# Scan layers: B's diagonals by DMA instead of DVE, bias and residual added by DVE out of PSUM

## The reference

```python
proj = seq @ W_proj.T + b_proj                    # x_in, delta, B, C
delta = softplus(delta + dt_bias);  A = -exp(A_log)
h = exp(d_t[..., None] * A) * h + (d_t * x_t)[..., None] * b_t[:, None, :]   # for every pixel t
y_t = einsum('bdn,bn->bd', h, c_t)
out = (y + x_in * D) @ W_out.T + b_out
x = x + out
```

## Time and profile before

| | |
|---|---|
| median of the runs | 4305.36 us |
| the profiled execution: span, first to last instruction | 4308.6 us |
| PE busy | 3710.7 us, 86% |
| DVE busy | 3432.3 us, 80% |
| POOL busy | 2659.4 us, 62% |
| ACT busy | 2105.8 us, 49% |
| DVE: diagonals (1160) | 454.0 us, 128 instructions |
| DVE: scans (1136) | 944.3 + 887.2 us, 1536 instructions |
| PE: scan inputs (818) | 865.7 us, 24576 matmuls |
| PE: sums over states (831) | 798.1 us, 3072 matmuls |
| transfers, mean of the span | 97 GB/s |

### The profile page before, as it was taken

One profiled execution on the slowest core, in us unless ns is written; L12 is line 12 of the kernel. 1 busy time (PEld: TensorE's weight loads), 2 busy tenths in 40 slices (PEclk: granted clock), 3 DMA queues, 4 the chain that ended last, 5 costly groups with the idle time before them and its releaser, 6 DMA issues.

```text
span 4308.6 us, 119610 instructions
## 1 busy us (share of the span) xinstructions
PE 3710.7 (86%) x49136; PEld 2266.0 (53%) x49136; DVE 3432.3 (80%) x3492; ACT 2105.8 (49%) x2803; POOL 2659.4 (62%) x973
## 2 busy tenths in 40 slices
PE   4994899899999996789889888899898888888897
PEld 4994666666666664344444444444444444444443
DVE  6564567667576663699998998999999989999997
ACT  2331343444444443556555555555565555555563
POOL 1111121111211210599899999999999999999998
PEclk9997899999999998799999999999999999999999
DMA  9624142242332330553543543544535535435433
GB/s 101 85 44 108 54 124 81 85 119 70 95 109 69 105 91 25 120 116 79 125 106 83 125 102 92 125 94 103 122 84 120 112 79 124 109 79 130 103 87 83
DMA packets 296948, 416.40 MB, mean 97 GB/s; under 512 B 31369, under 2 KB 185741, under 8 KB 296385
## 3 DMA queue, kind: packets, MB, share of 16 engines
q1 hardware_dynamic: 295440, 408.35, 41.7%
q10 hardware_dynamic: 978, 0.34, 0.0%
HBM read 267.09 MB, written 91.16 MB: 83 GB/s over the span
## 4 chain that ended last, share of the span: by engine, by line
PE 27%; DVE 16%; issue 12%; ACT 3%; POOL 1%; DVEq 1%; DMA 0%; ACTq 0%; POOLq 0%
DVE ssm_h L1136 11%; PE ssm_u_ps L818 10%; PE ssm_y_ps L831 10%; PE ssm_scratch L848 4%; DVE ssm_b_diag L1160 3%; PE ssm_scratch L858 1%; DVE ssm_stats L1143 1%; POOL ssm_h L1216 1%; ACT ssm_decay L967 1%; PE ssm_u_ps L893 1%; DVE ssm_y_sb L1165 1%; ACT ssm_xn L994 1%; PE ssm_scratch L873 1%; PE ssm_scratch L867 0%; DVEq L1128 0%
## 5 line engine op out<-in xcount | busy, mean ns | idle before, releaser
L1216 POOL TENSOR_TENSOR ssm_h<-ssm_h,ssm_c_rep 128x2048 f32<-128x2048 f32 x384 | 1745.4, 4550 | 107.3 <-DVE ssm_h L1136 99.6
L967 ACT ACTIVATE ssm_decay<-ssm_delta_rep,ssm_a_neg 128x1024 f32<-128x1024 f32 x768 | 863.7, 1145 | 592.1 <-DVE ssm_h L1136 589.3
L818 PE MATMUL ssm_u_ps<-ssm_b_diag,ssm_dx_t 64*64 64x128 f32 x24576 | 865.7, 282 | 262.3 <-DVE ssm_h L1136 182.6
L818 PEld LDWEIGHTS ssm_u_ps<-ssm_b_diag,ssm_dx_t 64*64 64x64 f32 x24576 | 696.3, 137 | 698.9 <-issue 694.6
L1136 DVE TENSOR_TENSOR_SCAN ssm_h<-ssm_decay,ssm_h,ssm_u_ps 128x512 f32<-128x512 f32 x768 | 944.3, 1257 | 132.5 <-PE ssm_u_ps L818 131.4
L1136 DVE TENSOR_TENSOR_SCAN ssm_h<-ssm_decay,ssm_u_ps 128x512 f32<-128x512 f32 x768 | 887.2, 1195 | 35.8 <-ACT ssm_decay L967 16.9
L831 PE MATMUL ssm_y_ps<-ssm_h,ssm_state_sum 128*64 128x512 f32 x3072 | 798.1, 643 | 8.0 <-POOL ssm_h L1216 8.0
L1752 ACT ACTIVATE l_probs<-l_work 128x532 f32<-128x532 f32 (+1 forms) x384 | 217.6, 567 | 560.7 <-PE l_work L1606 554.0
L1160 DVE TENSOR_TENSOR ssm_b_diag<-ssm_b_t,ssm_lane 128x2048 f32<-128x2048 f32 x128 | 454.0, 3549 | 22.7 <-ACT ssm_b_t L1022 22.7
L2004 POOL TENSOR_TENSOR l_rstd<-l_var_eps,l_minus_half 96x2 f32<-96x2 f32 x16 | 11.1, 695 | 586.6 <-DVE l_var_eps L1841 586.6
L831 PEld LDWEIGHTS ssm_y_ps<-ssm_h,ssm_state_sum 128*64 128x64 f32 x3072 | 196.8, 144 | 326.3 <-issue 311.9
(11 more groups left out here) (163 smaller groups left out, 5554.7 us busy)
## 6 DMA issues: line engine op xcount, KB each, us to landing
ssm_c_rep<-ssm_c_by_state SPq DMA_DIRECT2D x256, 512.0 KB, 6.5
ssm_delta_rep<-ssm_delta SPq DMA_DIRECT2D x384, 128.0 KB, 5.9
l_qk_parts<-l_qk SPq DMA_DIRECT2D x48, 768.0 KB, 4.8
ssm_x<-x_after_l SPq DMA_DIRECT2D x32, 768.0 KB, 5.8
ssm_x_res<-x_after_l SPq DMA_DIRECT2D x192, 128.0 KB, 4.3
l_x<-x SPq DMA_DIRECT2D x64, 192.0 KB, 9.1
x_after_l<-l_x SPq DMA_DIRECT2D x64, 192.0 KB, 4.1
l_x<-x_after_l SPq DMA_DIRECT2D x16, 768.0 KB, 5.5
```

Of the source, the lines that this page charges most:

```text
L818: made = nc.tensor.matmul(u_ps[64 * par:64 * par + 64, ring("u", w), r, at:at + 128], dx_t[rows, db, 2 * win + k, 64 * g:64 * g + 64], b_d ...
L967: nc.scalar.activation(decay[:, 2 * (s % 2) + npi, :], delta_rep[:, db, :], ACT.Exp, scale=a_neg[:, n.layer, col:col + 1]).then_inc(decay_ ...
L1216: nc.gpsimd.tensor_tensor(view, view, c_rep[:, 2 * q:2 * q + 2, :], ALU.mult).then_inc(c_applied, 1)
```

## The change

DVE no longer makes the diagonals. ACT writes B's transposes to a smaller `b_t` in another order. SP stores `b_t` to DRAM into the first 32 numbers of rows that are 544 numbers long and otherwise zero (they are cleared once at the start, by a transfer that ACT's queue issues). Read back in pieces of 512 numbers, each row of 544 shifts by 32 against its partition, so partition p of a block of 16 gets its B at column group p and zeros elsewhere: a diagonal. Eight such transfers of 16 partitions (32 KB each) fill one `b_diag[:, npq]`; blocks beyond the diagonal are zeroed once by DVE at the start. `b_diag` is now [partition, group, 64 columns, 32], and the moving operand of a matmul is 64 pairs of numbers, 128 bytes from pair to pair, where it was 128 numbers in a row.

`take_output` of ACT and `o_sb` are gone. DVE adds bias and residual straight from PSUM, with two instructions per output third, at the end of windows 7, 10 and 13; this add also frees the ring's slot.

```diff
-        b_diag = sb("b_diag", [128, 4, 8, 2, 128])
+        b_diag = sb("b_diag", [128, 4, 64, 32])
+        b_dram = nc.dram_tensor(f"{tag}_b_blocks", [4, 128, BLOCK * 32 + 32], F32).ap()     # BLOCK = 16
 # await_place: who frees an output's slot
-                eng.wait_ge(out_taken, before(n).count(3, USES[use][1] + 1))
+                eng.wait_ge(res_added, before(n).count(3, USES[use][1] + 1))
+        def of_part(npq, rows, win, k, g, par):
+            first = 16 * win + 8 * k + 4 * g + 2 * par
+            return b_diag[rows, npq, :, first:first + 2]
 # SP
+                def store_b(n):
+                    if not n.first:
+                        for npq in range(4):
+                            sp.wait_ge(diag_loaded[npq], n.count(128, 0))
+                            sp.sem_inc(b_store_seen, 1)
+                    sp.wait_ge(b_kept, n.count(1, 1))
+                    sp.dma_start(b_dram[:, :, 0:32].rearrange("q p v -> p q v"), b_t[:, :, :]).then_inc(b_stored, 16)
+                def load_diagonal(n, npq):
+                    if not n.first:
+                        sp.wait_ge(u_filled, before(n).count(8 * S_STEPS, 8 * (8 + npq) + 8))
+                        sp.sem_inc(diag_read, 1)
+                    flat_rows = b_dram[npq].rearrange("p v -> (p v)")
+                    for blk in range(128 // BLOCK):
+                        first = blk * BLOCK * (BLOCK * 32 + 32)
+                        j0 = BLOCK * blk % 64
+                        sp.dma_start(b_diag[BLOCK * blk:BLOCK * (blk + 1), npq, j0:j0 + BLOCK, :].rearrange("p j v -> p (j v)"),
+                                     flat_rows[first:first + BLOCK * BLOCK * 32].rearrange("(p v) -> p v", p=BLOCK)
+                                     ).then_inc(diag_loaded[npq], 16)
 # SP, late
                         store_c(m)
                         load_delta(m, 0)
+                        store_b(m)
                         sp.wait_ge(c_stored, m.count(32, 32))
+                        sp.wait_ge(b_stored, m.count(16, 16))
+                        load_diagonal(m, 0)
                         load_c(m, 0)
+                        load_diagonal(m, 1)
                         sp.wait_ge(decay_made, n.count(TILES_S, 16))
                         load_delta(m, 1)
+                        load_diagonal(m, 2)
                         load_c(m, 1)
+                        load_diagonal(m, 3)
 # PE, fill_u
-                        pe.wait_ge(diag_made, n.count(4, npq + 1))
+                        pe.wait_ge(diag_loaded[npq], n.count(128, 128))
-                                                            b_diag[rows, npq, 4 * win + 2 * k + g, par, :], start=True, stop=True)
+                                                            of_part(npq, rows, win, k, g, par), start=True, stop=True)
 # ACT, take_b
-                    nc.scalar.activation(b_t[:, :], scratch[:, 0:256], ACT.Copy).then_inc(drained, 1)
+                    nc.scalar.activation(b_t[:, :, :].rearrange("p q (c i) -> p q c i", i=2),
+                                         scratch[:, 0:256].rearrange("p (c z q i) -> p z q c i", z=2, q=4, i=2)[:, 0],
+                                         ACT.Copy).then_inc(drained, 1)
+                    await_drained(act, f)
+                    act.sem_inc(b_kept, 1)
 # DVE
+                def add_residual(n, q):
...
+                    dve.wait_ge(out_filled, n.count(3, q + 1))
+                    for a in range(2):
+                        rows = x_res[:, q, 256 * a:256 * a + 256].rearrange("p (g z) -> p g z", g=2)
+                        made = nc.vector.scalar_tensor_tensor(rows, u_ps[:, ring("out", q), :, 128 * a:128 * a + 128],
+                                                              b_out[n.layer][:, q:q + 1], rows, ALU.add, ALU.add)
+                    made.then_inc(res_added, 1)
 # DVE, window
                     scan(n, w // 2, w % 2, 0)
-                    if w in (17, 19, 21, 23) and not last:
-                        diagonals(after(n), w // 2 - 8)
                     scan(n, w // 2, w % 2, 1)
+                    if w - 2 in OUT_SLOTS and not n.first:
+                        add_residual(before(n), OUT_SLOTS.index(w - 2))
```

More of the change, by code:

```diff
@@ L580, in ssm_layers @@
         dx_made = sem("dx_made")
-        diag_made = sem("diag_made")
+        blocks_cleared = sem("blocks_cleared")
+        b_kept, b_stored, b_store_seen = sem("b_kept"), sem("b_stored"), sem("b_store_seen")
+        diag_read, diag_cleared = sem("diag_read"), sem("diag_cleared")
+        diag_loaded = [sem(f"diag_loaded{npq}") for npq in range(4)]
         rows_seen = sem("rows_seen")
@@ L1021, in take_b @@
                     await_fill(act, f)
[L1022 removed]
+                    if not n.first:
+                        act.wait_ge(b_stored, n.count(16, 0))
+                    nc.scalar.activation(b_t[:, :, :].rearrange("p q (c i) -> p q c i", i=2),
[3 more added lines that the diff above has]
+                    act.sem_inc(b_kept, 1)
                 def take_x(n, db):
@@ L1038, in take_dx @@
                                          ACT.Copy).then_inc(drained, 1)
-                def take_output(n, q):
-                    if q == 0 and not n.first:
-                        act.wait_ge(res_added, n.count(3, 0))
-                    if q == 0 and n.first:
-                        act.wait_ge(rest_loaded, 16 * N_REST)
-                    act.wait_ge(out_filled, n.count(3, q + 1))
-                    nc.scalar.activation(o_sb[:, q, :].rearrange("p (a g z) -> p a g z", a=2, g=2),
-                                         u_ps[:, ring("out", q), :, 0:256].rearrange("p g (a z) -> p a g z", a=2), ACT.Identity,
-                                         bias=b_out[n.layer][:, q:q + 1]).then_inc(out_taken, 1)
                 def take_slot(n, slot):
@@ L1065, in take_slot @@
                             take_dx(of, int(i))
-                    if slot in OUT_SLOTS and not n.first:
-                        take_output(before(n), OUT_SLOTS.index(slot))
                 def prologue(n):
@@ L1102, in tail @@
                 def tail(n):
-                    for q in range(3):
-                        take_output(n, q)
+                    pass
                 nc.scalar.preload_act_table_set("natural_log_exp_and_others")
@@ L1165, in keep_y @@
                     nc.vector.tensor_tensor(y_sb[:, n.s, db, :], y_ps[:, :], y_sb[:, n.s, db, :], ALU.add).then_inc(y_kept, 1)
+                def add_residual(n, q):
+                    if q == 0:
+                        dve.wait_ge(res_loaded, n.count(96, 96))
+                    if q == 0 and n.first:
+                        dve.wait_ge(rest_loaded, 16 * N_REST)
+                    dve.wait_ge(out_filled, n.count(3, q + 1))
[4 more added lines that the diff above has]
+                    made.then_inc(res_added, 1)
                 def prologue(n):
@@ L1175, in prologue @@
                     nc.vector.tensor_scalar(a_neg[:, :, :], a_neg[:, :, :], -1.0, None, ALU.mult).then_inc(consts_made, 1)
-                    for npq in range(4):
-                        diagonals(n, npq)
+                    nc.vector.memset(b_diag[:, :, :, :], 0.0).then_inc(diag_cleared, 1)
                 def window(n, w):
@@ L1204, in tail @@
                     keep_y(n, 2)
+                    for q in range(3):
+                        add_residual(n, q)
                 schedule(dve, prologue, early, late, tail)
@@ L1260, in step @@
                         power(after(n))
-                    if s in (3, 4, 6) and not n.first:
-                        add_residual(before(n), (3, 4, 6).index(s))
                     if not last:
@@ L1277, in tail @@
                 def tail(n):
-                    for q in range(3):
-                        add_residual(n, q)
+                    pass
                 pool.wait_ge(consts_made, 3)
@@ L2025, in shape_constants @@
     out["state_sum"] = (p[:, None] % 64 == np.arange(64)[None, :]).astype(np.float32)
-    out["lane"] = np.repeat(p[:, None] % 64 == np.arange(64)[None, :], 2, 1).astype(np.float32)
+    out["nothing"] = np.zeros((1, 4, BLOCK * 32 + 32), np.float32)
     out["ones"] = np.ones((1, 2, 2, 512), np.float32)
```

34 lines of the change are left out of this document (15 added, 19 removed).

## The result

The changed kernel takes 4204.5 us, the median of four runs (4197.08 to 4211.27), and the kernel before 4306.09 beside it: ratio 0.9758, 95% interval 0.9744 to 0.9771. It is 102 us faster; the forecast was 285.

A forecast was written before the change was run, and what follows sets the result against it. The diagonals on DVE were taken to bound the kernel, then PE: 31 x (79.42 - 70.0) = 292 won, 7 lost, span 4308.6 to 4023.6, less 3.2 for the median: 4020 us, range 3980 to 4240.

The forecast's parts named there:

- What bounds the kernel before: the diagonals on DVE: Scan layers: four diagonals a pass, 3.55 us each on DVE, delay all three engines; removing them frees 14.2 us of DVE.
- Next bound is PE, a pass of 70.0: Scan layers: PE's products sum to 67.3 us a pass, over DVE's 62.0 and POOL's 63.0; with extras 70.0.
- the allowance: PE's pass: 1.0 us added for the norm's small products and for waits between engines at nearly equal load.
- Bias and residual on DVE, 0.40 us each: Outputs: six DVE instructions a pass add 2.4 us; POOL loses three sums, 3.8 us; the new wait costs nothing.
- Strided reads cost nothing: 24 input products a pass: reading B as 64 pairs leaves each at 1.03 us; bounds no change to twice the time.
- The row with runs of four: Convolution's matmul, operand in runs of four 64 bytes apart: 118 ns per 128 columns, taken to show jumps cost nothing.
- the second rival: Input products: pairs slow the matmuls, at twice the time 94.7 us a pass and 4787 us in all; chance 0.14.
- Diagonals are hidden, with 1.3 to 2.6 us to spare: SP's transfers at a pass's end: 0.37 us issue each, 3.3 landing; each diagonal arrives 1.3 to 2.6 us early.
- The forecast's own rule: Late diagonals on SP: lateness of the last adds to the pass; 4.2 us late gives 74.2 a pass, 4151 us.
- Rival 1: SP becomes late: at 0.67 us per transfer a pass takes 78.0, the kernel 4269; range 4080 to 4270, chance 0.24.
- The transfers' fixed cost paid one after another: Diagonals' 32 loads a pass: 64 us instead of 12, the pass 120; set aside because fixed parts overlap.
- Ends: Once per kernel: prologue loses 8 us (0 to 15) to store, loads and clearing; tail wins 1 us.

The follow-up runs named there:

- both costs taken away: Changed kernel reading 128 consecutive numbers of B instead of pairs, with diagonals loaded in the first pass only (wrong numbers of B): 4023.9 us.
- the first part: Run alone: changed kernel with diagonals by DMA, but ACT evicting the outputs and POOL adding the residual as before the change: 4323.38 us, ratio 1.0040.

## Why the prediction was wrong, point by point

- *What bounds the kernel before: the diagonals on DVE.* Right. They went, and with them the 3.82 us wait and POOL's stretching; DVE and POOL came out within 1 us of the forecast.
- *Next bound is PE, a pass of 70.0.* Right as a sum: 70.18 with both costs taken away. In passes 2 to 29 of that run PE is busy 67.4 us a pass and idle 2.4, where the forecast had 67.3 and 2.7. The norm's products and waits were well covered by the allowance.
- *Bias and residual on DVE, 0.40 us each.* Measured 0.468, in the bounds and harmless. That this part is worth little, and only through POOL, was wrong: alone it gave 34 us, and it starts SP's stores 5.2 us earlier, without which the first part loses. I counted the chain from the third output's add, as the change has it, and never asked where the add of before stands.
- *Strided reads cost nothing.* Wrong, 0.1 us a product, 2.4 us a pass. The row with runs of four did not carry over to pairs; the bounds (1 to 2 times) held it, at a tenth of the way, so that the second rival was real in kind and far too dear.
- *Diagonals are hidden, with 1.3 to 2.6 us to spare.* This is the step that failed, and most of the loss. In us from the first store, medians of passes 4 to 28 of the changed kernel; "there" is the landing of a diagonal's last transfer, and "asked" is when PE asks for it in the kernel without loads, where nothing delays PE:

| diagonal | 0 | 1 | 2 | 3 |
|---|---|---|---|---|
| issued, forecast | 21.4 | 25.7 | 32.4 | 36.7 |
| issued, measured | 22.1 | 28.3 | 35.8 | 41.1 |
| there, forecast | 24.7 | 29.0 | 35.7 | 40.0 |
| there, measured | 23.5 | 32.4 | 37.3 | 46.6 |
| asked, forecast | 27.3 | 31.2 | 37.0 | 41.6 |
| asked, measured | 28.1 | 32.2 | 38.1 | 43.4 |

The asking times were right within 2 us, and diagonal 0 came earlier than forecast. Two terms failed. The issue: a transfer took 0.46 us and not 0.37, so that with the gaps between them the last diagonal was issued 4.4 us late. The landing: the forecast had 3.3 us for every transfer, which is nearly the median of all (3.2), but none of the four has it. Those of diagonals 0 and 2 land 1.8 us after their issue and those of 1 and 3, behind C's copies, after 5.2 and 5.4 (medians), over the end of 4.8 that the forecast had named. C's copies are there at 30.4 and 43.7 us, and the first transfers of diagonals 1 and 3 at 29.8 and 43.3, so these land with the copies and not on their own. No run moved the copies, so this cause is argued from the times. The margins became 4.6, -0.2, 0.8 and -3.1. PE waited accordingly: in the later passes not at all for diagonals 0 and 2, 12.4 us in 14 waits for 1, and 55.8 us in 24 waits for 3; the other 10.7 of the 78.9 us lie in the first pass.

A wait was also priced at its length. The waits that the profile names come to 2.5 us a pass, and SP's chain costs 4.1. The clock is part of the difference: in the 8 us behind a wait its mean is below 1 (2.4 GHz) after 16 of the 24 waits for diagonal 3, and after none of the 14 for diagonal 1. The forecast's own rule, which for a last diagonal 4.2 us late gives 4151 us, falls 45 us short even of the kernel that reads no pairs (4195.53).

- *Rival 1* had the right kind of loss, and its range held the time, with a chance of 0.24. The stated range held it only because it took in most of this rival: the pass is 76.08, outside the 69 to 72 of the forecast. A margin that I had called thin, worked out from one duration of another stage's loads, should have had more.
- *The transfers' fixed cost paid one after another* (an estimate of 64 us, from the 2 us that the Trainium skill, "DMA: Bandwidth & Descriptors", gives in its section on the anatomy of one DMA, fitted there to transfers that GpSimd issues): not so here, and that page does not say that it adds up. Eight transfers of a diagonal are issued in 3.6 us, and the last lands 1.4 to 5.2 us after that.
- *Ends.* 8 us lost in the prologue: the first scan came only 0.9 later (1764.19), but the first pass took 86.7 instead of 80.5, waiting up to 5.5 us for loads; 7.1 in all. The last pass was to win 1 and lost 3.5; 24 x 0.1 = 2.4 of it is, by estimate, the pairs, which it reads too.

## What to carry to other kernels

When work moves from an engine to transfers, write the chain of the issuing queue beside the times at which the data is asked for. Take each landing from what stands ahead of it in the queue, not from one median: here 1.8 and 5.2 us lay behind a median of 3.2. Where the margin does not hold, count a wait, and price it with the slow clock that can follow it, not by its length alone. While such a chain sets the pass, a faster engine only waits longer: of the 82 us that shorter products were to give, 9 came until SP was early. Two parts of a change can pay only together, and the part that looks small may be the one that starts the queue.

## What the hardware showed unexpectedly

Transfers of 32 KB and 128 KB cost SP's queue about the same issue (medians of 0.42 us each, 0.46 and 0.43 to 0.57 with the gap). The same transfer of 32 KB landed after 1.8 us, or after 5.2 to 5.4 us where it stood right behind two copies of 512 KB. A moving operand of pairs costs 0.01, 0.035 or 0.1 us per 32 matmuls at 64, 16 and 128 bytes, where runs of four at 128 bytes are free.
